# The last 96 gate and up rows of the experts and the shared expert as one 64+64 product and one 32+32 product in token halves

## The reference, cut to what matters

```python
E = 8
H = 352
...
h = jax.nn.silu(jnp.einsum('ecd,edh->ech', xd, W1)) * jnp.einsum('ecd,edh->ech', xd, W3)
oe = jnp.einsum('ech,ehd->ecd', h, W2).reshape(E * C, d)
out = jnp.take(oe, jnp.minimum(flat, E * C - 1), axis=0)
out = out * (gate * keep.astype(x.dtype))[:, None]
shared = jax.nn.silu(xt @ sw1) * (xt @ sw3) @ sw2
return (out + shared).reshape(b, sl, d)
```

## Time and profile before

| what | value |
|---|---|
| median of 3 runs | 513.6 us (512.69 to 515.35) |
| the profiled execution, its own time | 514.35 us |
| its span, first to last instruction | 512.5 us |
| PE busy | 475.1 us, 93% of the span |
| DVE busy | 381.3 us, 74% |
| ACT busy | 244.8 us, 48% |
| POOL busy | 231.1 us, 45% |
| mean granted TensorE clock | 0.993 |

### The profile page before, as it was taken

The page is one execution under the profiler, slowest core; times in us unless marked ns, Lnnn a source line. Parts: engine busy times, 40 slices in busy tenths (PEclk is TensorE's granted clock), DMA queues, the critical chain, the costliest instruction groups (busy, mean ns, idle before and its releaser), DMA issues. The chain is left out here.

```text
span 512.5 us, 10279 instructions
## 1 busy us (share of the span) xinstructions
PE 475.1 (93%) x3384; PEld 259.5 (51%) x3384; DVE 381.3 (74%) x764; ACT 244.8 (48%) x461; POOL 231.1 (45%) x321
## 2 busy tenths in 40 slices
PE   2898999998999989997999999898999999999993
PEld 2663664844733623343434433333444646788882
DVE  4979889899888699997899999999546643333331
ACT  2751232322231088896899899877512011233331
POOL 3737434154754166766676776313010560042433
PEclk9999999999999999999999999999999999999998
DMA  7750185002775025556556766600013125378853
GB/s 239 209 174 0 25 180 90 2 0 61 193 179 133 5 75 155 155 148 161 153 154 177 171 179 149 157 8 6 1 59 110 63 103 165 119 166 210 188 114 41
DMA packets 67256, 59.96 MB, mean 117 GB/s; under 512 B 10048, under 2 KB 62256, under 8 KB 67216
## 3 DMA queue, kind: packets, MB, share of 16 engines
q1 hardware_dynamic: 63712, 55.24, 39.5%
q0 software_dynamic: 3072, 4.21, 4.9%
q10 hardware_dynamic: 432, 0.00, 0.0%
HBM read 38.90 MB, written 22.50 MB: 120 GB/s over the span
## 5 line engine op out<-in xcount | busy, mean ns | idle before, releaser
L1308 DVE TENSOR_REDUCE MX<-psum 128x2 f32<-128x512 f32 x256 | 162.5, 683 | 12.7 <-PE psum L1173 10.9
L1357 ACT ACTIVATE HP<-psum 128x512 f32<-128x512 f32 x224 | 122.2, 601 | 37.1 <-PE psum L1188 34.7
L1173 PE MATMUL psum<-QKA 60*128 60x256 bf16 x512 | 82.4, 275 | 8.3 <-DVE MX L1308 4.6
L1188 PE MATMUL psum<-QKA 60*128 60x256 bf16 x512 | 81.4, 275 | 1.8 <-DMA QKA<-max_scr 1.0
L1274 PE MATMUL psum<-HP,VP 128*32 128x256 f32 x1024 | 82.6, 394 | 0.2 <-issue 0.2
L588 PE MATMUL psum<-space_a,space_w 128*128 128x512 f32 x160 | 73.1, 602 | 2.8 <-DVE HP L615 2.0
L1173 PEld LDWEIGHTS psum<-QKA 60*128 60x128 bf16 x512 | 32.2, 95 | 65.5 <-DVE MX L1308 42.6
L1933 POOL DMA_INDIRECT out_x<-OE,to_u x16 | 24.9, 1557 | 62.6 <-ACT OE L1968 60.1
L588 PEld LDWEIGHTS psum<-space_a,space_w 128*128 128x128 f32 x160 | 29.0, 190 | 37.4 <-issue 31.9
L2056 PE MATMUL psum<-XT,WE 128*128 128x256 f32 (+1 forms) x192 | 44.0, 379 | 0.9 <-ACT XT L1952 0.9
L199 PE MATMUL psum<-space_a,wsh 128*128 128x512 f32 (+1 forms) x96 | 43.6, 598 | 0.3 <-PEq L1480 0.3
(11 more groups left out here) (203 smaller groups left out, 766.5 us busy)
## 6 DMA issues: line engine op xcount, KB each, us to landing
QKA<-stack_scr SPq DMA_DIRECT2D x32, 480.0 KB, 4.6
stack_scr<-PARTS SPq DMA_DIRECT2D x32, 192.0 KB, 2.4
WE<-in_W SPq DMA_DIRECT2D x16, 352.0 KB
stack_scr<-PARTS SPq DMA_DIRECT2D x32, 128.0 KB, 2.1
XD<-dispatched SPq DMA_DIRECT2D x8, 258.0 KB, 4.0
X<-in_x SPq DMA_DIRECT2D x4, 512.0 KB, 5.7
CTX<-in_ctx SPq DMA_DIRECT2D x4, 512.0 KB, 8.0
MB<-in_mask SPq DMA_DIRECT2D x16, 128.0 KB, 3.0
```

The source lines that it names most:

```text
L1173: return pe.matmul(to[:, tt * T:(tt + 1) * T], QKA[rows, k, 0, h, tt * P:(tt + 1) * P], QKA[rows, k, 1, h, :], start=True, stop=True)
L1188: return pe.matmul(to[:, (m % 2) * T:(m % 2 + 1) * T], QKA[rows, k, 1, h, st * P:(st + 1) * P], QKA[rows, k, 0, h, :], start=True, stop=True)
L1308: dve.tensor_reduce(MX[:, par, head_of(n), :], src[:, :].rearrange("p (a s) -> p a s", a=2), axis=AX.X, op=ALU.max).then_inc(a_red, 1)
L1357: act.activation(PT[:, i % 2, st, 2 * half:2 * half + 2, :].rearrange("p j t -> p (j t)"), TBK3[THIRDS[m]], ACT.Exp).then_inc(a_exp, 1)
```

## The change

The third piece is cut otherwise. Of its 96 gate and 96 up rows, the first 64 of each are put side by side as the 128 columns of one weight tile: one product gives 64 gate rows on partitions 0 to 63 and 64 up rows on 64 to 127 of one bank. The last 32 of each form a weight tile of 64 columns. Its product is made for each half of the tokens apart, the first half on partitions 0 to 63, the second on 64 to 127 of a second bank. ACT and DVE work on the third piece in three parts in place of one: 64 rows over all tokens, and 32 rows over each half. The weights are loaded into tiles laid out for this, so that gate and up weights of the experts come in six transfers in place of two, and those of the shared expert in six in place of two. The other pieces stay as they were.

```diff
+WIDE, NARROW = 64, 32
+REST = (NH - 1) * P
...
+        def gate_up_pieces(main, rest, gate_w, up_w):
+            for side, w in enumerate((gate_w, up_w)):
+                yield main[:, side, :, :], w[:, :, 0:REST]
+                yield rest[:, :, WIDE * side:WIDE * (side + 1)], w[:, :, REST:REST + WIDE]
+                lo = 2 * WIDE + NARROW * side
+                yield rest[:, :, lo:lo + NARROW], w[:, :, REST + WIDE:EH]
+        def gate_up_rest(pe, w, side, to, of, n):
+            for h in range(2):
+                if side == 0:
+                    last = pe.matmul(to[:, 0:n], w[:, h, 0:2 * WIDE], of(h, 0, n), start=(h == 0), stop=(h == 1))
+                    continue
+                for f in range(2):
+                    last = pe.matmul(to[2 * NARROW * f:2 * NARROW * (f + 1), 0:n // 2], w[:, h, 2 * WIDE:2 * (EH - REST)],
+                                     of(h, n // 2 * f, n // 2 * (f + 1)), start=(h == 0), stop=(h == 1))
+            return last
+        def rest_parts(a, b, n):
+            half = n // 2
+            yield slice(0, WIDE), slice(0, n), a[0:WIDE, 0:n], a[WIDE:2 * WIDE, 0:n]
+            for f in range(2):
+                lo = 2 * NARROW * f
+                yield (slice(WIDE, WIDE + NARROW), slice(half * f, half * (f + 1)),
+                       b[lo:lo + NARROW, 0:half], b[lo + NARROW:lo + 2 * NARROW, 0:half])
...
+            if i == NH - 1:
+                for rows, n, gate_in, _ in rest_parts(bank[2 * i], bank[2 * i + 1], GT):
+                    last = act.activation(THS[rows, i, n], gate_in, ACT.Tanh, scale=0.5)
+                last.then_inc(m_th, 1)
+                return
...
+                for rows, n, gate_in, _ in parts:
+                    ch.do(ch.eng.scalar_tensor_tensor(out=H1S[rows, i, n], in0=THS[rows, i, n], scalar=1.0,
+                                                      in1=gate_in, op0=ALU.add, op1=ALU.mult))
+                ch.wait()
+                for rows, n, _, up_in in parts:
+                    last = ch.eng.scalar_tensor_tensor(out=HS[rows, g % 2, i, n], in0=H1S[rows, i, n], scalar=0.5,
+                                                       in1=up_in, op0=ALU.mult, op1=ALU.mult)
+                last.then_inc(m_h, 1)
+                return
...
-                        for dst, src in ((WE1[:, s, :, :], W1), (WE3[:, s, :, :], W3)):
-                            sp.dma_start(dst, src[bass.ds(e, 1), :, :].rearrange("e (h p) i -> p (e h) i", p=P))\
-                              .then_inc(e_w[s], 16)
+                        for dst, src in gate_up_pieces(WE13[:, s, :, :, :], WER[:, s, :, :],
+                                                       *(w[bass.ds(e, 1), :, :].rearrange("e (h p) i -> p (e h) i", p=P)
+                                                         for w in (W1, W3))):
+                            sp.dma_start(dst, src).then_inc(e_w[s], 16)
...
-                            pe.wait_ge(e_w[s], 64 * (e2 + 1))
+                            pe.wait_ge(e_w[s], 128 * (e2 + 1))
...
+                        if i == NH - 1:
+                            for side in range(2):
+                                last = gate_up_rest(pe, WER[:, s, :, :], side, bank[i + side],
+                                                    lambda h, lo, hi: XT[:, s, h, lo:hi], CAP)
+                            last.then_inc(e_gu, 1)
+                            return
```

More of the change, by code:

```diff
@@ L197, in gu_shared @@
                 pe.wait_ge(m_h, NH * (g - 1) + i + 1)
+            if i == NH - 1:
+                last = gate_up_rest(pe, wshr, side, bank[2 * i + side],
+                                    lambda h, lo, hi: ZT4[:, h, bass.ds(GT * g + lo, hi - lo)], GT)
+                if side == 1:
+                    last.then_inc(m_gu, 1)
+                return
             for h in range(2):
-                last = pe.matmul(bank[2 * i + side][0:m, :], (wsh1, wsh3)[side][:, h, i * P:i * P + m],
+                last = pe.matmul(bank[2 * i + side][0:m, :], wsh13[:, side, h, i * P:i * P + m],
                                  ZT4[:, h, bass.ds(GT * g, GT)], start=(h == 0), stop=(h == 1))
@@ L213, in hidden_shared @@
             ch.eng.wait_ge(m_th, NH * g + i + 1)
+            if i == NH - 1:
+                parts = list(rest_parts(bank[2 * i], bank[2 * i + 1], GT))
+                for rows, n, gate_in, _ in parts:
[7 more added lines that the diff above has]
+                return
             ch.do(ch.eng.scalar_tensor_tensor(out=H1S[0:m, i, :], in0=THS[0:m, i, :], scalar=1.0,
@@ L825, in _ @@
                     for dst, src in ((wgt[:, :, 0:NE], Wg.rearrange("(h p) e -> p h e", p=P)),
[L826 to L827 removed]
+                                     *gate_up_pieces(wsh13, wshr, *(w.rearrange("(h p) e -> p h e", p=P) for w in (sw1, sw3))),
                                      (wsh2[:, 0:2, :], sw2[0:2 * P, :].rearrange("(i p) c -> p i c", p=P)),
@@ L1958, in tanh_expert @@
                             act.wait_ge(e_h, NH * (e - 1) + i + 1)
+                        if i == NH - 1:
+                            for rows, n, gate_in, _ in rest_parts(bank[i], bank[i + 1], CAP):
+                                last = act.activation(TH[rows, i, n], gate_in, ACT.Tanh, scale=0.5)
+                            last.then_inc(e_th, 1)
+                            return
                         act.activation(TH[0:m, i, 0:CAP], bank[i][0:m, 0:CAP], ACT.Tanh, scale=0.5).then_inc(e_th, 1)
@@ L2050, in gu_expert @@
                             pe.wait_ge(e_xt, e + 1)
-                            pe.wait_ge(e_w[s], 64 * (e2 + 1))
+                            pe.wait_ge(e_w[s], 128 * (e2 + 1))
                         if not first:
                             pe.wait_ge(e_h, NH * (e - 1) + i + 1)
-                        for w, lo in ((WE1, 0), (WE3, CAP)):
+                        if i == NH - 1:
+                            for side in range(2):
+                                last = gate_up_rest(pe, WER[:, s, :, :], side, bank[i + side],
+                                                    lambda h, lo, hi: XT[:, s, h, lo:hi], CAP)
+                            last.then_inc(e_gu, 1)
+                            return
+                        for side, lo in ((0, 0), (1, CAP)):
                             for h in range(2):
-                                last = pe.matmul(bank[i][0:m, lo:lo + CAP], w[:, s, h, i * P:i * P + m],
+                                last = pe.matmul(bank[i][0:m, lo:lo + CAP], WE13[:, s, side, h, i * P:i * P + m],
                                                  XT[:, s, h, :], start=(h == 0), stop=(h == 1))
@@ L2216, in hidden_expert @@
                         dve.wait_ge(e_th, NH * e + i + 1)
+                        if i == NH - 1:
+                            parts = list(rest_parts(bank[i], bank[i + 1], CAP))
+                            for rows, n, gate_in, _ in parts:
+                                ch.do(dve.scalar_tensor_tensor(out=H1[rows, i, n], in0=TH[rows, i, n], scalar=1.0,
+                                                               in1=gate_in, op0=ALU.add, op1=ALU.mult))
+                            ch.wait()
+                            for rows, n, _, up_in in parts:
+                                last = dve.scalar_tensor_tensor(out=HE[rows, i, n], in0=H1[rows, i, n], scalar=0.5,
+                                                                in1=up_in, op0=ALU.mult, op1=ALU.mult)
+                            last.then_inc(e_h, 1)
+                            return
                         ch.do(dve.scalar_tensor_tensor(out=H1[0:m, i, 0:CAP], in0=TH[0:m, i, 0:CAP], scalar=1.0,
```

10 lines of the change are left out of this document (5 added, 5 removed).

## The result

The changed kernel takes 525.31 us, the median of 6 runs (522.54 to 528.36), against 513.68 us for six runs of the kernel before on the same chip (512.69 to 515.62). The ratio is 1.0217, with a 95% interval of 1.0176 to 1.0257. The forecast of 515.3 us was wrong, and so was its range, which ended at 518.9. The profiled run took 523.45 us, with a span of 521.5 us and a mean granted clock of 0.990.

What follows compares the result with a forecast made beforehand. PE, busy 93% of the span, was taken as the bound, with DVE setting group 1's wait. -0.64 - 1.02 - 0.25 + 1.2 + 1.0 + 1.4 = +1.7 us on 513.6 gave 515.3 us, range 512.8 to 518.9.

Steps and rivals of the forecast that it cites:

- PE's saving: Third-piece matmuls: narrow products run in pairs, saving 0.08 us per expert and 0.51 per shared group; 1.9 us in all.
- the 0.25 of group 0: Shared expert's group 0: PE's block end comes 0.51 us earlier, but DVE then sets the end, so 0.25 us gained.
- The rival that the halves run unpaired: Third piece's narrow matmuls run one by one, so each visit costs 0.34 us: 520.6 us in all, chance 0.06.
- Transfers: Gate and up weight loads: six transfers and smaller packets lengthen the load from 1.9 to 2.4 us, costed at nothing.
- The rival of 1.0 to 1.9 us in every turn: Small weight packets delay W2, so PE waits for each of six experts: +6 to +11 us, chance 0.07.
- The first step that failed: Third-piece parts overlap on ACT and DVE: 0.72 us on ACT, 0.84 per DVE step, 1.2 us more in all.
- -0.64 + 1.2 + 1.0 = 1.6: Experts: -0.64 us PE saving over eight, +1.2 for waits in experts 1 to 6, +1.0 for expert 7's wait.
- the 1.4 forecast: Shared group 1: two DVE hidden steps in three parts make the rows PE waits for 1.4 us later.
- the last of the prediction's own signs of being wrong: The forecast is wrong if ACT's and DVE's small parts take clearly more than 0.9 us a step.
- The first rival: Parts don't overlap on ACT and DVE; PE waits 0.65 us in six turns, 1.5 at the end: 518.8 us, chance 0.13.
- the bound for the parts: Upper bound on an expert's added ACT and DVE time, at 0.34 us per 128-column DVE instruction: 1.5 us, against 1.2.
- The second step that failed: Shared groups 2 and 3: over 5 us of other PE work covers the later hidden rows, so they cost nothing.

Runs made afterwards that it cites:

- e2: Changed kernel with ACT and DVE taking the third piece in one part of 96 rows (other values): 512.66 us, ratio 0.9969.
- e3: Kernel before with every gate and up weight loaded in pieces of 256, 64 and 32 columns: 514.09 us, ratio 1.0010.
- e7: Changed kernel with every expert's down products taking first and second pieces for both token tiles, then the third: 522.09 us, ratio 1.0147.
- e8: e7 with the shared expert's down products also reordered, third pieces after the first two of all four token tiles: 515.26 us, ratio 1.0027.
- e11: e8 with the last expert's third piece put ahead of its second on all engines: 515.21 us, ratio 1.0023.
- e1: Kernel before with only the third piece's tanh and hidden steps on ACT and DVE cut in three: 521.97 us, ratio 1.0134.
- e10: Changed kernel with GpSimd's sixteen scatters held back until group 1's third hidden rows are there: 524.07 us, single run.
- e4: Changed kernel run again, unaltered, for a second trace: 525.01 us, ratio 1.0206 to the kernel before.
- e5: Kernel before with only the shared expert's third piece as in the changed kernel: 520.05 us, ratio 1.0104.
- e6: Kernel before with only the experts' third piece as in the changed kernel: 518.60 us, ratio 1.0077.
- e12: e5 with the shared expert's down products in e8's order, experts as in the kernel before: 513.42 us, ratio 0.9979.

## Why the prediction was wrong

**PE's saving: right.** The narrow products run in pairs at the cost forecast. In e2 an expert's turn is 0.08 us shorter, as forecast, and groups 2 and 3 together 1.12 us for the 1.02 forecast. The next block's first product begins 0.33 us after DVE's last instruction of the attention (379.37 - 379.04) in place of 0.60 (380.73 - 380.13), the 0.25 of group 0. The rival that the halves run unpaired falls.

**Transfers: right, but by little.** e3 costs 0.1% with an interval that holds no change, and no trace of the changed kernel or of e3 shows PE waiting for WE. e2 does, 0.47 us once in six turns of 8.14; e7, e8 and e11, with the same loads and turns of 8.13, do not. The rival of 1.0 to 1.9 us in every turn falls; a cost of nothing held in the changed kernel's longer turns and is at its edge in turns of 8.14.

**The first step that failed** is "I take 0.08 off each but the last on DVE and 0.10 on ACT". The overlap was read from full instructions of 508 and 512 columns that lie on the same first rows. The parts lie on different rows and overlap by nothing: ACT 0.93 us for the 0.72 forecast, DVE 1.04 and 1.02 for 0.84 twice. From ACT's start to the weight load it is 468.80 - 465.69 = 3.11 us for the 2.5 to 2.8 forecast. A turn therefore grew by 0.56 us net where 0.12 was forecast, and the experts by 5.1 us in all where -0.64 + 1.2 + 1.0 = 1.6 was forecast. In group 1 the two steps take 1.57 and 1.56 us, and the rows came 1.57 + 1.56 - 2 x 0.68 = 1.77 us later for the 1.4 forecast. The small parts thus took clearly more than 0.9 us a step, the last of the prediction's own signs of being wrong. The first rival had these sizes (0.65 a turn, 1.5 at the end, 1.7 in group 1), and got a chance of 0.13. The Trainium skill (Advanced Engine Details and Errata, The Read-Write Bubble) had spoken for it: it says that memory latency shows as a bubble between instructions, and advises large tiles to keep that overhead small. The trace agrees with it for the changed kernel's parts, 1.04 us for three of 0.98 in sum. e1 sets a bound to it: two parts on the same rows still overlap by about 0.1 us. Three slips in the sums change little: the bound for the parts is 1.4 us, not 1.5 (0.05 more on four instructions), the new load 2.5 us, not 2.4, and an expert's saving 0.09, not 0.08.

**The second step that failed** is "Groups 2 and 3 have over 5 us of other PE work before the rows are needed: nothing". The cover, PE's work between that piece's products and the products that need its rows, is 16 matmuls of 0.43 us, 6.9 us, but I counted it against the parts' length alone. Their start was late by 5 us as well, and so PE waited 2.55 us. e10 and e8 show when: a tanh can start late if its products end in the last 8 us or so before SP's token load, that is, late in GpSimd's scatters. Before, it started 6.7 us ahead of that load (423.04 - 416.33); group 1's wait had moved the end of its products to 3.9 us ahead (421.53 - 417.60). Why the counts are held then stays open (below). No rival had this.

**What no step had:** half the clock behind a wait. It cost 1.7 us behind group 1's wait, in both traces of the changed kernel, and as much again behind the second one in the trace of e4.

The first rival's 518.8 us, and on top of it 1.7 us of clock, the wait of 2.55 us and in some runs 1.7 us more, give 523.1 to 524.8; 525.3 was measured. e5 and e6 carry this: the halves of the change cost 1.0% and 0.8%, the whole 2.2%, and the intervals cover the difference. e8 takes the shared expert's two waits, the lost clock and the turns' waits away by order alone, and returns to 1.0027. What the last expert loses, some 1.5 us, was read from the traces and not removed by any run.

## What to carry to other kernels

Count an instruction cut in three at the sum of three full lengths, as here, unless a trace shows such parts overlapping on such rows; multiply that by the steps between one engine's product and the next product that reads it. Before splitting such a piece, look for products that don't need it and put them ahead of the wait: with the down products in another order the same change costs 0.3% in place of 2.2%, and its shared half alone gains 0.2% (0.01 to 0.40). A cover read from one profile holds only for that moment; if something ahead comes later, ask what else goes on by then.

## What the runs showed of the hardware

**Counts that arrive late while scatters end.** In all 13 profiles a tanh whose products had ended up to 6.6 us earlier starts 0.85 to 1.18 us after SP issues the token load, which waits for the last scatter. The delay from the products' end is 5.0 us in the changed kernel, 4.3 in e10 (430.60 - 426.32) and 6.6 in e5 (421.62 - 414.97). In four profiles (before, e6, e10, e12) an earlier tanh of the same stretch got through in between, in e12 2.5 and in e6 2.9 us late. It is the count that is late, not ACT: the changed kernel's trace records the count of group 2's third piece at 422.51 us and that of group 3's first at 422.61, though their products end at 417.60 and 421.24. PE's own matmuls go on at full pace meanwhile. What holds the counts is not settled; only that it moves with the scatters was shown.

**Half the clock behind a wait is not certain.** The same wait of 1.88 us (1.89 in e10) with the same work around it was followed by a granted clock of 0.51 in the changed kernel (6.28 us for 20 matmuls, likewise in e4, e7 and e10) and by full clock in e5 (4.60 us). Behind the second wait it stayed full in the changed kernel (2.55 us) and halved in e4 (2.55 us), in e5 (4.19 us) and in e1 (3.69 us). What decides between the two was not tried.
